# Attention 0: products one unit later, projections together, ScalarE's copies ahead of its exponentials

## The reference

```
h    = layernorm(x) * (1 + ca) + sa            # ca, sa, ga: rows from silu(c) @ wmod, one set per sequence
xn   = rms_norm(h)
q, k, v = split(xn @ w_qkv.T)                  # 16 heads of 64
q, k = rope(q), rope(k)                        # x1*cos - x2*sin, x2*cos + x1*sin
attn = q @ k.T / 8, masked to q_pos - 32 <= k_pos <= q_pos
out  = softmax(attn) @ v
x    = x + ga * (out @ w_out.T)
```

## Time and profile before

| | us |
|---|---|
| median of three runs | 1290.49 |
| lowest, highest | 1288.48, 1291.82 |
| span of the profiled execution, first to last instruction (nothing outside it is recorded) | 1295.1 |
| TensorE, VectorE, ScalarE, GpSimd busy in the span | 975.8, 805.3, 639.2, 430.4 |

### The profile page before, as it was taken

How to read it: one execution, slowest core, us unless ns; L and a number is a source line. 1 busy time by engine, 2 the same in 40 slices (tenths; PEclk the granted TensorE clock), 3 DMA queues, 4 the chain that set the end, 5 groups by cost and what they waited for, 6 DMA issues and landing times. The chain is left out here.

```text
span 1295.1 us, 25137 instructions
## 1 busy us (share of the span) xinstructions
PE 975.8 (75%) x8604; PEld 662.5 (51%) x8604; DVE 805.3 (62%) x1683; ACT 639.2 (49%) x2132; POOL 430.4 (33%) x332
## 2 busy tenths in 40 slices
PE   6779998989899999985613769747348787867665
PEld 3456565656656565664503556534225454545454
DVE  5777758687777767564657514112136878559995
ACT  3565767767676767671101323112038777643322
POOL 2334333333342423321000857886611312200221
PEclk9789899999999998987555789888759999868967
DMA  6564343434443434431402123445310000000000
GB/s 198 150 182 107 92 123 88 119 96 113 102 113 100 113 83 107 104 91 42 102 0 62 45 59 69 61 73 129 31 66 1 1 2 1 1 1 9 17 17 25
DMA packets 89009, 93.62 MB, mean 72 GB/s; under 512 B 18800, under 2 KB 62304, under 8 KB 88944
## 3 DMA queue, kind: packets, MB, share of 16 engines
q1 hardware_dynamic: 78576, 84.12, 24.7%
q0 software_dynamic: 10368, 8.66, 4.7%
HBM read 24.36 MB, written 10.70 MB: 27 GB/s over the span
## 5 line engine op out<-in xcount | busy, mean ns | idle before, releaser
L835 POOL TENSOR_TENSOR qk_cos<-qk_raw,const 128x512 f32<-128x512 f32 x128 | 183.2, 1432 | 313.0 <-ACT qk_raw L589 313.0
L575 ACT ACTIVATE prob<-psS,neg_max 128x96 f32<-128x96 f32 x512 | 167.9, 342 | 86.5 <-DVE neg_max L670 85.7
L442 PE MATMUL psQ<-a_xnT,weights 128*128 128x512 f32 x250 | 146.0, 668 | 2.1 <-ACT a_xnT L621 1.4
L550 PEld LDWEIGHTS psO<-probT,v_windows 96*64 96x64 f32 x2048 | 73.7, 143 | 142.6 <-ACT probT L649 121.1
L550 PE MATMUL psO<-probT,v_windows 96*64 96x64 f32 x2048 | 91.8, 235 | 43.9 <-ACT probT L649 43.9
L685 DVE TENSOR_TENSOR qk_roped<-qk_cos,qk_swapped 128x512 f32<-128x512 f32 x128 | 119.0, 929 | 5.9 <-DVE qk_swapped L676 5.5
L1508 POOL DMA_INDIRECT sums<-ex_y,ex_index x64 | 97.6, 1525 | 39.5 <-issue 23.5
L1497 POOL DMA_INDIRECT ex_rows<-rows,ex_index x64 | 67.1, 1048 | 121.8 <-DMA ex_index<-lists 102.6
L575 ACT ACTIVATION_READ_ACCUMULATOR prob<-psS,neg_max 128x1 f32 x512 | 105.4, 206 | 0.0
L1442 ACT ACTIVATE ex_hidden<-ex_psH,ex_b 128x512 f32<-128x512 f32 x64 | 43.7, 687 | 114.4 <-PE ex_psH L1401 59.7
L649 ACT COPY probT<-psT 96x512 f32<-96x512 f32 x128 | 76.8, 600 | 46.5 <-PE psT L530 46.5
(11 more groups left out here) (317 smaller groups left out, 1936.2 us busy)
## 6 DMA issues: line engine op xcount, KB each, us to landing
qk_swapped<-qk_raw SPq DMA_DIRECT2D x512, 64.0 KB, 2.0
v_windows<-v_tok SPq DMA_DIRECT2D x32, 384.0 KB, 4.4
v_windows<-v_tok SPq DMA_DIRECT2D x32, 256.0 KB, 3.6
mod<-mod_rows SPq DMA_DIRECT2D x12, 512.0 KB, 6.0
ex_w<-in_L_ffn_W SPq DMA_DIRECT2D x16, 256.0 KB
v_windows<-v_tok SPq DMA_DIRECT2D x32, 96.0 KB, 2.1
rows<-rt_h SPq DMA_DIRECT2D x8, 256.0 KB, 2.4
sums<-rt_zeros SPq DMA_DIRECT2D x8, 256.0 KB, 2.7
```

The costliest lines, as they stand in the source:

```text
L442: last = nc.tensor.matmul(bank, k.wqkvT[:, col:col + P], xnT[:, :], start=True, stop=True)
L550: ins = nc.tensor.matmul(psO[D * j:D * j + D, i * P + a * HALF:i * P + (a + 1) * HALF], vw[:, par, a, t, hd], probT[:, 2 * j + i, a * HALF ...
L575: last = nc.scalar.activation(prob[:, s, 2 * j + i, :], psS[:, s, j, i * KW:(i + 1) * KW], ACT.Exp, bias=nmax[:, s, 2 * j + i:2 * j + i + ...
L835: nc.gpsimd.tensor_tensor(rcos[:, half, :], raw[:, half, :], k.const[:, K_COS:K_COS + T], ALU.mult).then_inc(cos_done, 1)
```

## The change

The products of a unit move one unit later on TensorE, and those of unit 15 between the two parts of the output product. A unit's projections follow one another, behind the products. ScalarE's order becomes: copy probT of u, the pieces of u-1, exponentials of u+2, copy oT of u-1. `probT` and `v_tok` get two buffers each, in memory of `k.mod1`, which isn't in use yet. The pieces are numbered anew, values last, and PLAN carries (0, 1), (2), (3, 4), (5). The cores of the diff:

```diff
-        v, vw = sb("v_tok", [P, TILES, 4 * D]), sb("v_windows", [KW, 2, 2, TILES, 4 * D])
+        spare = k.mod1[:, :, :, :].rearrange("p j b c -> p (j b c)")
+        v = spare[:, 0:2 * TILES * 4 * D].rearrange("p (h t d) -> p h t d", h=2, t=TILES)
+        probT = spare[0:KW, 2 * TILES * 4 * D:2 * TILES * 4 * D + 2 * 4 * P].rearrange("p (h i q) -> p h i q", h=2, i=4)
...
-        VALUE = (3, 5)
-        PLAN = ((0,), (1,), (2, 3), (4, 5))
+        VALUE = (4, 5)
+        PLAN = ((0, 1), (2,), (3, 4), (5,))
...
+            def apply(b, u):
+                g, t = divmod(u, TILES)
+                wait(pe, probT_ready, b * UNITS + u + 1)
+                wait(pe, oT_ready, b * UNITS + u)
+                if t == 0:
+                    wait(pe, v_placed[g % 2], b * 96 + (g // 2 + 1) * 48)
...
             def body(b, last):
                 for u in range(UNITS):
+                    turn_prob(b, u)
                     if not (last and u + 2 >= UNITS):
                         score(b, u + 2)
+                    if u > 0:
+                        apply(b, u - 1)
                     if u == 0:
                         wait(pe, y_read, b)
...
-                    for q, m in pieces[:1]:
+                    for q, m in pieces_at(u // TILES, u % TILES, last):
                         project(b, q, m)
...
                 out_project(b, list(range(PAIRS - 2)), True, False)
+                apply(b, UNITS - 1)
                 wait(pe, oT_ready, b * UNITS + UNITS)
                 out_project(b, [PAIRS - 2, PAIRS - 1], False, True)
...
             def body(b, last):                     # ScalarE
                 for u in range(UNITS):
-                    if u > 0:
-                        copy_oT(b, u - 1)
-                    wait(act, turned, b * UNITS + u + 1)
-                    nc.scalar.copy(probT[:, :, :], psT[0:KW, :, :]).then_inc(probT_ready, 1)
-                    for q, m in pieces[:1]:
-                        piece(b, q, m)
+                    copy_probT(b, u)
+                    if u > 0:
+                        pieces(b, u - 1, last)
+                    if u == 8 and not last:
+                        copy_xnT(b + 1)
                     if not (last and u + 2 >= UNITS):
                         exps(b, u + 2)
-                    for q, m in pieces[1:]:
-                        piece(b, q, m)
+                    if u > 0:
+                        copy_oT(b, u - 1)
                     if u == 4 and not last:
                         squares(b + 1)
-                    if u == 7 and not last:
-                        copy_xnT(b + 1)
+                pieces(b, UNITS - 1, last)
                 copy_oT(b, UNITS - 1)
...
-                wait(sp, piece_out, b * QUADS * PIECES + q * PIECES + ((1, 2, 3, 4) if first else (1, 2, 3, 5))[half])
+                wait(sp, piece_out, b * QUADS * PIECES + q * PIECES + half + 1)
...
-                sp.dma_start(vw[:, par, 1, :, :], v[P - KW:P, :, :]).then_inc(v_placed, 16)
+                sp.dma_start(vw[:, par, 1, :, :], v[P - KW:P, par, :, :]).then_inc(v_placed[par], 16)
```

More of the change, by code:

```diff
@@ L357, in phase_attention0 @@
         ONTO = [psQ[:, 0, :], psQ[:, 1, :], psO[:, :]]
-        OPENING = [(0, m) for m in (0, 1, 2, 4, 3, 5)] + ["wo0", "wo1"] + [(1, m) for m in (0, 1, 2, 4, 3, 5)]
+        OPENING = [(0, m) for m in range(PIECES)] + ["wo0", "wo1"] + [(1, m) for m in range(PIECES)]
         scored, turned, applied = sem("scored"), sem("turned"), sem("applied")
-        normed_ready, v_placed = sem("normed_ready"), sem("v_placed")
+        normed_ready, v_placed = sem("normed_ready"), [sem(f"v_placed{i}") for i in range(2)]
         projected, x_turned, y_ready = sem("projected"), sem("x_turned"), sem("y_ready")
@@ L439, in project_onto @@
                 if m not in VALUE:
-                    half = half_of(m)
-                    col = (half % 2) * H0 * D + (2 * g + half // 2) * P
+                    col = (m % 2) * H0 * D + (2 * g + m // 2) * P
                     last = nc.tensor.matmul(bank, k.wqkvT[:, col:col + P], xnT[:, :], start=True, stop=True)
@@ L509, in _ @@
                     pe.wait_ge(w_dve, 1)
-                if OPENING[n] == (0, 3):
+                if OPENING[n] == (0, VALUE[0]):
                     pe.wait_ge(w_act, 2)
@@ L519, in _, with turn_prob @@
             pe.wait_ge(w_act, 5)
+            def turn_prob(b, u):
+                wait(pe, probT_ready, b * UNITS + u)
+                wait(pe, normed_ready, b * UNITS + u + 1)
+                for i in range(4):
+                    ins = nc.tensor.transpose(psT[0:KW, i, :], prob[:, u % 2, i, :], k.ident)
+                ins.then_inc(turned, 1)
+            def apply(b, u):
[4 more added lines that the diff above has]
+                    wait(pe, v_placed[g % 2], b * 96 + (g // 2 + 1) * 48)
+                for i in range(2):
+                    for a in range(2):
+                        for j in range(2):
+                            hd = slice((2 * i + j) * D, (2 * i + j + 1) * D)
+                            ins = nc.tensor.matmul(psO[D * j:D * j + D, i * P + a * HALF:i * P + (a + 1) * HALF],
+                                                   vw[:, g % 2, a, t, hd], probT[:, u % 2, 2 * j + i, a * HALF:(a + 1) * HALF],
+                                                   start=True, stop=True, skip_group_check=True)
+                ins.then_inc(applied, 1)
             def body(b, last):
                 for u in range(UNITS):
[L523 to L531, removed]
+                    turn_prob(b, u)
                     if not (last and u + 2 >= UNITS):
                         score(b, u + 2)
-                    pieces = pieces_at(g, t, last)
+                    if u > 0:
+                        apply(b, u - 1)
                     if u == 0:
@@ L585, in piece_from @@
                 if m not in VALUE:
-                    half = half_of(m)
                     if not (isinstance(b, int) and b == 0 and q == 0):
-                        wait(act, roped, b * HALVES * QUADS + HALVES * (q - 1) + half + 1)
-                    ins = nc.scalar.copy(raw[:, half, :], bank)
+                        wait(act, roped, b * HALVES * QUADS + HALVES * (q - 1) + m + 1)
+                    ins = nc.scalar.copy(raw[:, m, :], bank)
                 else:
@@ L592, in piece_from @@
                     if first == 0:
-                        wait(act, v_placed, (b * QUADS + q) * 48)
-                    ins = nc.scalar.copy(v[:, first:first + 2, :], bank.rearrange("p (t d) -> p t d", t=2))
+                        wait(act, v_placed[q % 2], b * 96 + (q // 2) * 48)
+                    ins = nc.scalar.copy(v[:, q % 2, first:first + 2, :], bank.rearrange("p (t d) -> p t d", t=2))
                 ins.then_inc(piece_out, 1)
@@ L635, in _ @@
                 opening(n)
-                if OPENING[n] == (0, 4):
+                if OPENING[n] == (0, HALVES - 1):
                     copy_sixth(4)
@@ L641, in _, with copy_probT, pieces @@
                     exps(0, 1)
+            def copy_probT(b, u):
+                wait(act, turned, b * UNITS + u + 1)
+                nc.scalar.copy(probT[:, u % 2, :, :], psT[0:KW, :, :]).then_inc(probT_ready, 1)
+            def pieces(b, u, last):
+                for q, m in pieces_at(u // TILES, u % TILES, last):
+                    piece(b, q, m)
             def body(b, last):
                 for u in range(UNITS):
-                    g, t = divmod(u, TILES)
+                    copy_probT(b, u)
[3 more added lines that the diff above has]
+                        copy_xnT(b + 1)
+                    if not (last and u + 2 >= UNITS):
+                        exps(b, u + 2)
                     if u > 0:
                         copy_oT(b, u - 1)
-                    wait(act, turned, b * UNITS + u + 1)
-                    nc.scalar.copy(probT[:, :, :], psT[0:KW, :, :]).then_inc(probT_ready, 1)
-                    pieces = pieces_at(g, t, last)
-                    for q, m in pieces[:1]:
-                        piece(b, q, m)
-                    if not (last and u + 2 >= UNITS):
-                        exps(b, u + 2)
-                    for q, m in pieces[1:]:
-                        piece(b, q, m)
                     if u == 4 and not last:
                         squares(b + 1)
-                    if u == 7 and not last:
-                        copy_xnT(b + 1)
+                pieces(b, UNITS - 1, last)
                 copy_oT(b, UNITS - 1)
@@ L832, in cosines @@
             def cosines(b, q, half):
-                first = isinstance(b, int) and b == 0 and q < 2
-                wait(pool, piece_out, b * QUADS * PIECES + q * PIECES + ((1, 2, 3, 4) if first else (1, 2, 3, 5))[half])
+                wait(pool, piece_out, b * QUADS * PIECES + q * PIECES + half + 1)
                 nc.gpsimd.tensor_tensor(rcos[:, half, :], raw[:, half, :], k.const[:, K_COS:K_COS + T], ALU.mult).then_inc(cos_done, 1)
```

8 lines of the change are left out of this document (3 added, 5 removed).

## The result

The changed kernel takes 1319.83 us (median of four runs, 1318.4 to 1321.84) beside 1290.16, which is 29.7 more. The ratio on record is a little larger, 1.0255, with an interval of 1.0228 to 1.0282: 33 us on 1290. This text goes by the ratio; where it says 33 us, the two medians alone say 30. (Beside the later experiments the kernel before had medians of 1286.0 to 1288.6.) The kernel is slower, as forecast, but by more than the 19 us that were forecast and the 30 of its upper bound.

The account below looks back on a forecast made before the run. The VectorE-ScalarE loop, not TensorE, was taken as the bound. Terms -1.0 + 0.97 + 1.48 + 0.65 + 0.57 = +2.7 us per sequence, in seven of eight, +19 on 1290.49: 1309.5 us, range 1299 to 1321.

Parts of the forecast that it names:

- the loop: VectorE's maxima and ScalarE's exponentials wait for each other: 14.13 of 14.69 us per quad, so about 0.5 us to win.
- the way of the late swap: Later windows delay half 0's swaps to E(12)+7.85; sines wait 1.5 us. E(u): start of exponentials ScalarE issues in unit u.
- the cover: Unit 12's quad, kernel before: half 0's last swap lands at 316.3, sines begin at 317.72, 1.4 us to spare.
- The 1303 us: Whole time if 64 KB swaps take the skill's 2.15 us, not 2.5: sines wait 1.2 instead of 1.5 us.
- the start and the end of a sequence: First exponentials no longer behind a piece's copy, -0.77 us; unit 15's product and copy inside the output product, +0.57.
- y_mul to E(8): Sequence start through its first two quads, 34.65 us before: -1.0 us, bounds -1.4 and +0.3.
- E(8) to E(12): Steady quad of 14.69 us: +0.97, 0.5 gained from the loop and 1.5 lost to the late swap.
- E(12) to E(15): Quad of unit 12, 10.87 us before: 12.35, +1.48, and +0.65 for a cosine ahead of the rotation.
- E(4) to E(6): Second quad's first two units, with statistics and squares: 8.99 us becomes 9.04 plus a cosine, +0.25.
- a rival at 5% only: Cosines hit each quad and TensorE's clock doesn't keep 1.00: over 4.3 us per sequence, 1325 us; chance 5%.
- the ends: First sequence counted among the seven at +2.7 us; last sequence 0, bounds -3 and +2.
- My reading of the cosines: GpSimd's cosine ahead of a rotation makes it 1.32 us for 0.69: 0 to 1.0 per quad hit, 0.65 taken.

Follow-up runs that it names:

- short cosines: GpSimd's cosines cut to 64 of 512 columns from sequence 1 on: 1304.33 us in the changed kernel, 1271.48 us in the kernel before.
- early windows: Changed kernel with the oT copy ahead of the exponentials: 1297.57 us, ratio 1.0081; with cosines of 64 columns as well, 1270.42 us.

## Why the prediction was right in kind and wrong in size

**Right: the loop, not TensorE's waits, sets the pace.** The products' wait for probabilities went, as predicted, and the kernel became slower all the same; the products now wait for oT copies instead (45.8 us), and taking that wait away too (3.8 us, with the maximum ahead of the sines) left 1320. Where no swap is late, the intervals are 3.31, also from E(11) to E(12), where it was 3.82.

**Right: the way of the late swap.** Windows began within 0.1 us of the forecast, and the sines waited for the swap in three quads of each middle sequence. The gate moved alone, in the kernel before, brings more than the whole loss; the oT copy moved back takes two thirds of it away, though that run moves TensorE's and ScalarE's work as well. What the prediction didn't see is the second gate, the piece's later copy: it booked 6.9 for the landing without windows, and the run with windows in the third unit has 7.6, 7.3 and 6.5 in the three quads of one sequence.

**Wrong: which swap is the last.** This is the term of the sum that was mis-sized. The earlier trace rows names the transfer at 313.82 the last of the four swaps. It is the third; the fourth is issued at 314.45 and lands 2.2 us later, at 316.6. So the distance from the first window to the last landing is 6.4 us, not 6.1, and the cover was 1.1, not 1.4. The sines then start 8.1 us behind E(12), not 7.85. Where no cosine is in the way, two units take 9.27 to 9.30 for 9.04. At three such waits this is 0.75 us per sequence, most of the 0.9 by which the sum per sequence was short.

The Trainium skill ("DMA: Bandwidth & Descriptors", Anatomy of one DMA) states its fit for transfers that GpSimd issues, and these are SyncE's; by its figures 64 KB take an estimated 2.15 us. The fourth swap, which the sines wait for, took 2.2 us before and 2.1 after and agrees with it; the first three, nearer behind the windows, took 3.7, 3.3 and 2.5. The prediction set the fit aside for the 2.5 of the third. The 1303 us that it worked out by the fit came of putting 2.15 us behind the third swap's issue, so they say nothing against the page.

**Right: the start and the end of a sequence.** y_mul to E(0) fell from 2.57 to 1.79 (forecast -0.77). From E(15) to y_mul it is +0.76 (+0.57).

**Wrong in size: the sum per sequence, +2.7.** In the sequence at full clock it is 72.2 - 68.6 = 3.6. By the prediction's parts: y_mul to E(8) -0.9 (-1.0); E(8) to E(12) +1.2 (+0.97), the transfer's 0.25; E(12) to E(15) +2.5 (+1.48 and +0.65), of which 0.25 is the transfer's and 0.8 the cosines', at the rotation and at the sines; the end +0.75. Inside the first part E(4) to E(6) is +0.9 where I had booked +0.25: GpSimd's square root and three cosines crowd there, and one holds the sines. The first quad is +0.3 where I had booked +0.65.

**The clock: no term, and little in the sum.** I had it in a rival at 5% only. Four of the five sequences shown ran at 0.95, where four of the same five ran at 1.00 before. The fall can be placed. In the sequence that starts at 276 us, E(2) to E(4) is 8.6 us where the sequence at full clock has 7.1, and the tables of stretches there, and at the same place of the sequence at full clock, are:

```profile
282.00:285.00 3.00, 1.27 (x34) 0.95 (x34) 2.97 (x9) 2.24 (x11) 1.38 (x1) 1.00 0.43 107
285.00:288.00 3.00, 3.00 (x14) 1.72 (x10) 2.97 (x6) 2.05 (x10) 1.26 (x1) 0.55 0.39 97
```

```profile
355.67:358.67 3.00, 1.28 (x34) 0.95 (x34) 2.96 (x9) 2.25 (x11) 1.38 (x1) 1.00 0.43 107
358.67:361.67 3.00, 3.00 (x34) 2.12 (x32) 2.97 (x6) 2.31 (x11) 1.26 (x1) 1.00 0.38 96
```

TensorE is busy 1.3 of 3 us in both; behind it the granted clock was 0.55 in one and 1.00 in the other. So the gap alone doesn't decide whether the clock falls. In the four sequences at 0.95 the intervals with such a fall are 0.8 to 1.7 us longer in all than in the one at 1.00. But the kernel before has slower sequences too, 71.9 and 70.0 us, and over the six middle ones the change adds 22.4 where six times 3.6 would be 21.5. That leaves about 1 us for the clock in the whole.

**Wrong: the ends.** I took the first sequence as +2.7; its y_mul came 8.5 later. VectorE waits 13.0 us for swaps there from 40 us on (6.1 before), up to 6.1 at once, beside loads: the DMA engines are 81% busy from 80 to 100 us, 58% before. Part of the 8.5 is chance: with short cosines, where the first sequence is the same code in each pair, its y_mul comes at 126.9 for 125.2, only 1.7 later. With early windows it comes at 124.1. For the last I had taken 0 and it is +2.7; its one late swap makes E(4) to E(6) 10.2 us for 7.4. Of the 14.5 us between forecast and trace these two ends are 8.5. The middle six are the other 6: 4.5 are the mis-read swap, and the rest the cosines, the end and the clock. Why the first sequence loses more is not settled: no run took the loads away.

**My reading of the cosines was half right.** I had booked them as a cost that the change adds. In their places they are; but the kernel before paid as much elsewhere, as the pair with short cosines shows. Only with the windows early do they cost the changed kernel more (27 us beside 15).

## What to carry to other kernels

Before an instruction is moved within its engine's order, list the gates that hang on its semaphore: here a copy of 0.38 us was the gate of three transfers, and behind these in the same queue stood the one that was urgent. Set the delay against the cover: the transfers landed 1.1 us before they were wanted, and the gate moved by 2.9. When several transfers feed one instruction, look for the row of the last of them; here the third was taken for it. Then look for the next gate behind the one that is removed. And spread work evenly over the units first: that took 1% off, while taking TensorE's waits, which lie beside the loop, won nothing.

## What the runs showed that I had not expected

- A gap of 1 to 2 us ahead of a long product can be paid twice: behind gaps of 1.38 and 0.97 us the granted clock was 0.50 for 5 us, and 64 instructions took 9.29 us for 7.31. It isn't always so, as the two sequences above show.
- A VectorE instruction that is due while a GpSimd one runs ended about 0.54 us after it; alone it takes 0.69. This was so for sines and rotations and, with 0.41 for 0.56, for the division. Cutting GpSimd's instruction to an eighth of its columns took 15 us off both kernels. The Trainium skill ("GPSIMD Engine Reference", Specifications) says that GpSimd shares its SBUF interfaces with VectorE and contends with instructions of two SBUF inputs; the trace agrees.
